# A fused attention and feed-forward kernel on eight cores: key matmul ahead of V's, the norm in two parts, and matmuls that nobody reads in some attention steps

## What is computed

```python
q = rms_norm(heads(x @ Wq), q_g)            # 16 heads of 64, 32 of them used in scores
kv = x @ Wkv                                # latent of 128
k = rms_norm(heads(kv @ Wk), k_g); v = heads(kv @ Wv)   # 32 per head
p = softmax(causal(q[..., :32] @ k.T / 8))
x = layernorm(x + pad(p @ v) @ Wo)
gate = silu(bitlinear(x, w_gate)); up = bitlinear(x, w_up)
x = layernorm(x + bitlinear(gate * up, w_down))
# bitlinear: activations to int8 per row, weights to -1, 0, 1 by their mean magnitude
```

## Time and profile before

| | us |
|---|---|
| three timed runs, median (lowest to highest) | 1638.44 (1637.69 to 1682.19) |
| the profiled execution, its own time | 1643.48 |
| its slowest core's span (core 6) | 1641.9 |
| spans of the eight cores | 1625.1 to 1641.9 |
| granted TensorE clock, mean of a core | 0.851 to 0.858 |

### The profile page before, as it was taken

The page is one execution under the profiler, slowest core; times in us unless marked ns, Lnnn a source line. Parts: engine busy times, 40 slices in busy tenths (PEclk is TensorE's granted clock), DMA queues, the critical chain, the costliest instruction groups (busy, mean ns, idle before and its releaser), DMA issues.

```text
span 1641.9 us, 22928 instructions; the slowest of 8 cores (1625.1 to 1641.9 us)
## 1 busy us (share of the span) xinstructions
PE 1302.4 (79%) x7494; PEld 438.3 (27%) x7494; DVE 806.2 (49%) x1158; ACT 824.7 (50%) x998; POOL 317.9 (19%) x350
## 2 busy tenths in 40 slices
PE   1676675788666888979869898989868999898966
PEld 0221121122111222222212222222223444343422
DVE  2227875468447766143561434143347762635522
ACT  2577564878784676657546686768601210111100
POOL 1024412033020304121123003130220020202021
PEclk8876686567556998989979998999989999898978
DMA  9995765779595785523255232523165585765646
GB/s 249 275 274 168 224 213 192 172 250 276 188 272 191 259 231 157 130 80 101 85 159 130 90 91 73 159 81 105 60 179 197 176 209 189 169 206 155 187 138 159
DMA packets 146514, 283.07 MB, mean 172 GB/s; under 512 B 91744, under 2 KB 92000, under 8 KB 133088
## 3 DMA queue, kind: packets, MB, share of 16 engines
q1 hardware_dynamic: 144816, 272.70, 54.6%
q0 software_dynamic: 1584, 8.91, 3.5%
HBM read 235.96 MB, written 33.55 MB: 164 GB/s over the span
## 4 chain that ended last, share of the span: by engine, by line
PE 51%; DVE 18%; issue 11%; ACT 8%; DMA 7%; POOL 3%; SPq 1%; DVEq 1%; ACTq 0%; POOLq 0%
PE ps_w L986 14%; PE ps_w L1109 6%; PE ps_sc L827 6%; ACT PT L840 5%; PE ps_den L782 4%; PE ps_sc L986 4%; PE ps_pv L793 3%; PE ps_sc L1109 3%; DVE S L775 3%; DMA R<-scr_w 2%; PE ps_w L547 2%; DVE st L690 2%; DMA R<-R 2%; DVE qb L382 2%; PE ps_w L714 2%
## 5 line engine op out<-in xcount | busy, mean ns | idle before, releaser
L840 ACT ACTIVATE PT<-ps_sc,negM 128x1024 bf16<-128x1024 f32 (+3 forms) x640 | 592.7, 983 | 197.6 <-PE ps_sc L827 195.3
L986 PE MATMUL ps_w<-R,S 128*128 128x512 fp8e4 x1280 | 336.1, 393 | 34.0 <-DVE R L1005 20.3
L827 PE MATMUL ps_sc<-qn,khat 32*128 32x512 bf16 (+3 forms) x1280 | 200.4, 397 | 63.5 <-ACT PT L840 58.7
L848 POOL TENSOR_TENSOR PT<-PT,tri 128x512 bf16<-128x512 bf16 x64 | 80.3, 1254 | 530.4 <-ACT PT L840 528.7
L986 PEld LDWEIGHTS ps_w<-R,S 128*128 128x128 bf16 x1280 | 106.4, 99 | 210.2 <-issue 121.0
L782 PE MATMUL ps_den<-PT,ones 128*32 128x512 bf16 (+3 forms) x1280 | 131.7, 402 | 18.4 <-DVE S L771 10.3
L853 POOL TENSOR_SCALAR PT<-PT,hflag_sb 128x512 bf16<-128x512 bf16 x64 | 112.9, 1763 | 111.0 <-ACT PT L840 110.9
L793 PE MATMUL ps_pv<-PT,vtok 128*32 128x512 bf16 (+3 forms) x1280 | 130.6, 398 | 0.1
L1109 PE MATMUL ps_w<-R 128*128 128x512 fp8e4 x416 | 114.2, 401 | 14.1 <-DMA R<-R 11.2
L986 PE MATMUL ps_sc<-R,S 128*128 128x512 fp8e4 x512 | 116.3, 386 | 8.8 <-DMA R<-scr_w 8.7
L1005 DVE SCALAR_TENSOR_TENSOR R<-R,ps_w 128x512 f32<-128x512 f32 x80 | 54.8, 685 | 137.2 <-ACT R L999 137.2
(11 more groups left out here) (182 smaller groups left out, 1379.2 us busy)
## 6 DMA issues: line engine op xcount, KB each, us to landing
R<-scr_w SPq DMA_DIRECT2D x192, 512.0 KB, 4.5
R<-wffn SPq DMA_DIRECT2D x69, 1024.0 KB, 7.6
scr_w<-qb SPq DMA_DIRECT2D x48, 256.0 KB, 6.6
khat<-wffn SPq DMA_DIRECT2D x9, 1024.0 KB, 15.0
vtok<-wffn SPq DMA_DIRECT2D x9, 1024.0 KB, 7.8
R<-xt POOLq DMA_DIRECT2D x7, 1024.0 KB, 13.7
R<-scr_x SPq DMA_DIRECT2D x12, 512.0 KB, 5.8
y<-R SPq DMA_DIRECT2D x12, 512.0 KB, 7.4
```

What stands on the lines that cost most here:

```text
L827: t = pe(lambda e, j=j, gi=gi, tc=tc, kc=kc, stc=stc: e.matmul(ps_sc[:, j * 512 + stc:j * 512 + 512], khat[32 * j:32 * j + 32, kc:kc + 128 ...
L840: t = act(lambda e, hf=hf, pp=pp, stc=stc: e.activation(PTr[pp][:, 2 * hf:2 * hf + 2, stc:512], PSr[:, 2 * hf:2 * hf + 2, stc:512], AF.Exp ...
L848: t = pool(lambda e, pp=pp, stc=stc: e.tensor_tensor(PTr[pp][:, :, stc:stc + 128], PTr[pp][:, :, stc:stc + 128], tri.rearrange("p (r n) -> ...
L986: t = pe(lambda e, c=c, b=b, kw=kk[w], i=i: e.matmul(wring.bufs[b], xqT[u % 2][:, i * 1024 + c * 128:i * 1024 + c * 128 + 128], wbuf[kw][: ...
```

## The change

Four edits in the program that writes the queues:

1. In `keys_values2` K's matmul and its squares come first and V's matmul behind it, in the same stage. V's copy to vtok is issued behind both.
2. In `projections` the last part of the job before (the writing of khat or qn, which frees the held bank) is issued ahead of the next job's first stage, where it stood behind it.
3. In `wo_ln1` the norm is split. The statistics are a piece of their own, and the normalization goes with the quantization. With two pieces per step, a row tile now takes four steps where it took three.
4. A helper `idle_mms` issues matmuls with the constant `bd32` on the first 512 columns of qn, into a free bank of `wring`, that nothing reads: four after each attention step that follows a stage of `keys_values2`, until the next stage of `queries2` or the one of `latent2` has run, and three per step between the end of the projections and the start of the feed-forward.

```diff
@@ keys_values2(c5, hc)
             kb = kvT[c5 % 2]
+            b1 = wring.take()
+            p1 = wring.bufs[b1]
+            t1 = pe(lambda e: e.matmul(
+                p1, wk[:, hc * 128:(hc + 1) * 128], kb, start=True, stop=True),
+                [t_kv[c5], wring.free[b1]], True)
+            t_sq = squares([(t1, p1)])
             b3 = wring.take()
             p3 = wring.bufs[b3]
-            t3 = pe(lambda e: e.matmul(
+            t3 = t_last[c5] = pe(lambda e: e.matmul(
                 p3, kb[:, hc * 128:(hc + 1) * 128], wv, start=True, stop=True),
-                [t_kv[c5], wring.free[b3]], True)
+                [wring.free[b3]], True)
...
             wring.give(b3, ends["v"])
-            b1 = wring.take()
-            p1 = wring.bufs[b1]
-            t1 = t_last[c5] = pe(lambda e: e.matmul(
-                p1, wk[:, hc * 128:(hc + 1) * 128], kb, start=True, stop=True),
-                [wring.free[b1]], True)
-            t_sq = squares([(t1, p1)])
             yield
@@ projections()
                 for _ in range(stages):
-                    next(job)
                     if old is not None:
                         next(old, None)
                         old = None
+                    next(job)
+                    st["few"] = stages == 2
                     yield
@@ wo_ln1(ti)
-            def norm1():
-                t_rs = layernorm_stats([state[0], state[1]], 0)
+            def stats():
+                state["rs"] = layernorm_stats([state[0], state[1]], 0)
+
+            def norm1_quant():
                 state["n"] = dve(lambda e: e.tensor_scalar(
-                    rt, rt, mv[:, 0:1], mv[:, 2:3], ALU.subtract, ALU.mult), [t_rs])
-
-            def quant():
+                    rt, rt, mv[:, 0:1], mv[:, 2:3], ALU.subtract, ALU.mult), [state["rs"]])
...
-            return [lambda: project(0), lambda: project(1), norm1, quant, None, store]
+            return [lambda: project(0), lambda: project(1), stats, None, norm1_quant, None, store,
+                    None]
@@ ahead of attention()
+        def idle_mms(n):
...
+            w = wring.take()
+            for _ in range(n):
+                pe(lambda e: e.matmul(wring.bufs[w], bd32[:], qn[:, 0:512], start=True,
+                                      stop=True), [wring.free[w]])
+            wring.give(w, wring.free[w])
@@ the main loop
         for part in attention():
             if not st["proj"]:
+                if st["few"]:
+                    idle_mms(4)
                 next(proj_it, None)
+            elif not ffn_on[0]:
+                idle_mms(3)
```

More of the change, by code:

```diff
@@ L311, in build_nc @@
         st = {"proj": False, "load": 0, "item": 0, "q": 0, "scl": None, "sum": [], "junk": None, "fi": None,
-              "mean": None}
+              "mean": None, "few": False}
         def stream_prefetch():
```

## The result

The changed kernel takes 1671.1 us (median of 4 runs, 1668.3 to 1713.9) where the one before takes 1641.4 (median of 4, the three above and one more). One execution of each kernel (1713.9 and 1682.2 us) was in a slower state of the chip, and the ratio leaves them out. It is 1.018, 95% interval 1.014 to 1.022: slower by about 30 us, where 1614 had been forecast, with a range up to 1640. The clock did rise as forecast: the cores' means lay between 0.851 and 0.858 and lie between 0.889 and 0.899 now. The time did not follow it.

A forecast was written before the change was run, and what follows sets the result against it. No engine was full over the whole span, so the bound was sought by stretch (ACT, DVE, or waits). Terms -8 - 12 + 2 - 3 + 3 + 9 - 7 - 8 = -24 us gave 1614 from the median 1638.4; range 1586 to 1640.

The forecast's parts named there:

- Edits 1 and 2: K and V jobs: K's matmul no longer waits for V's copy, so short waits go; -8 us, bounds 0 and 47.3.
- The third rival: K and V steps: the clock doesn't rise and PE becomes the bound; +13, 1651 us; chance 0.10.
- the wait changed its name: First rival, at K's matmul: it waits for khat instead of V's copy; total gain only -10, 1628 us; chance 0.27.
- inputs were ready a step earlier: At K's matmul: khat of the job before can be written without delay; ground for the -8 us.
- Edit 3, first tile: Stretch 260.9 to 299.5 us: the split norm ends 8.7 us of POOL waits and 3 us of blocks; -12 us.
- The wait of 8.80: K's matmul in the stretch of waits, with V's copy behind a norm on DVE; forecast to be gone.
- the last norm ahead of a chain: Pieces don't fit into 13 steps, so one norm runs right ahead of a chain; +2 us, bounds 0 and about 7.
- Edit 3, third tile: Feed-forward running, from step 204: 28 matmuls fall behind and are done alone after the attention; +3 us, bounds 0 and +7.
- Start of the feed-forward: Waits of 10.95 and 5.35 us for DVE at 527.13 and 540.85; half of 16.3 goes, -8 us, bounds 0 and -16.
- The gain of a warm start: Query matmuls and output projections after K and V parts start at full clock: 5 us and 2, together -7.
- The price: Unread matmuls at the low clock after about seven long DVE waits, one to two steps each: 7 x 1.3 = +9 us.
- at the full clock the fillers are hidden behind ACT or DVE: K and V steps with four fillers: 2.6 us of PE work per step against 3.8 us that ACT needs.

The follow-up runs named there:

- norm only: The kernel before with the split norm (edit 3) as its only change; ratio 0.995 (0.993 to 0.998), 1632.9 us.

## Why the prediction was wrong

**Edits 1 and 2: the failed step.** The prediction says "Edit 1 and 2, K's matmul first and khat's writing ahead. K's matmul now waits for khat of the job before". The edit in `projections` is made for every job, and I worked it out for one kind. Query and latent jobs had no reason to wait: their first matmuls used the free bank. Ahead of them the edit takes an overlap away and gives nothing. There was no term for it, nor a rival; it is 39 us (1671.1 against 1631.9 us with that part undone), and without it the change would have been faster, as forecast in sign, but by 8 us and not by 24. The third rival was slower too, at 1651, by a clock that stays low; the clock rose, so its reason isn't the one.

For the K and V jobs themselves I took -8 us; it was -3 (ratio 0.998), and the wait changed its name, 63.0 us for V's copy and khat to 59.4 for khat and qn. The argument that khat's "inputs were ready a step earlier" was wrong in some of the cases that it was made for: in eight of them DVE stood idle until ACT's exponential was done, 0.94 us ahead of K's matmul. In the long cases the inputs were ready and DVE was late, as I had said.

**Edit 3, first tile.** The wait of 8.80 isn't gone, but shorter: K's matmul at the same step waited 5.46 us with the norm alone (core 2) and 3.73 in the changed kernel. The one of 6.36, two steps ahead of it, became 0.94 with the norm alone. So this mechanism was right in kind. The POOL waits of the norms fell. The source of the norm's first instruction in the changed kernel (L730), then in the one before (L727):

```profile
  POOL mv L697: 9.8, 9
```

```profile
  POOL mv L696: 25.9, 16
```

Of the 12 us forecast, steps 34 to 49 gave 6.9 (norm only), and the last norm ahead of a chain cost 3.6 where I took 2. Together with the latent order that grew to 8.6: the profile shows DVE's block and the matmul that waited for its end (timeline of the changed kernel, DVE rows and a PE row):

```profile
310.70 1.27 DVE L691 BATCH_NORM_STATS2 st<-r_t 128x6 f32<-128x512 f32 x2
...
317.47 0.69 DVE L739 TENSOR_SCALAR S<-S 128x1024 bf16<-128x1024 f32 x1 [0.17 <-DVE S L737]
318.08 0.68 DVE L773 TENSOR_SCALAR S<-ps_den 128x512 f32<-128x512 f32 x1
...
323.34 0.68 DVE L582 TENSOR_TENSOR khat<-ps_w,S 128x512 bf16<-128x512 f32 x1
```

```profile
324.16 1.86 PE L528 MATMUL ps_w<-R 128*128 128x512 bf16 x4 [9.32 <-DVE khat L582]
```

The block runs from 310.70 to 324.0, and a latent's matmul, which in the old order would have run beside it, waited 9.32 us for its last instruction.

**Edit 3, third tile.** I forecast +3. With the norm alone, on core 0, steps 195 to 260 took 193.5 us instead of 218.3, steps 260 to 319 5.2 us more and what follows 6.4 more: -13 together. The eight cores lie between -3 and -16 there, with -7 in the middle; the sign holds on all of them, the size doesn't. That the 28 matmuls are done later fits the last two numbers. What I hadn't counted is the gain while they are missing. Whether it is the shorter DVE blocks or the steps without feed-forward work I didn't try apart.

**Start of the feed-forward.** Forecast -8. Steps 108 to 112 gave 8.6 us (norm only), and steps 112 to 124 took 8.4 back, since one of the norms now lies there: nothing.

**Edit 4.** The clock rose as expected, to 0.69 to 0.84 where it had been 0.50 to 0.60 in the table's stretches (0.83 from step 49 to 91, after 0.62 from 299.5 to 458 us), and the first query matmuls after K and V steps ran at 1.89 instead of 3.57. The gain of a warm start, taken as 7, was larger: with the unread matmuls alone -6.4 us at the queries on core 0 (-9.2 in the middle of the cores) where I took 5, and -6.9 at the feed-forward's start, which I had not counted; the 2 us of the last stretch ahead of it didn't come. The price, taken as +9, was 26 us, and the net +14 against +2. The failed step is "at the full clock the fillers are hidden behind ACT or DVE": it compared sums per step, 2.6 us of PE against 3.8 of ACT, and not the place. In steps 91 to 108, with three per step and PE's own work of 1.30, they cost 8.5 us as well, and 4.2 with one per step. I expect the waits of an output projection's additions and the low clock at the start of it to be the cause, and haven't tested that.

By the rule of the Trainium skill that I had set beside this ("TensorE: Matmul & The Clock Gate", "Part 1: The HAM clock gate"), a busy array gets the full clock. The traces agree: with the unread matmuls the mean was 0.885 to 0.897, and half as many left it at 0.863 to 0.872; all of them behind the stage, where they waited, left it at 0.862 to 0.874. What a full clock is worth is another question, and here it was worth less than its price. That there is nothing between the two levels holds in the traces of the kernel before and the changed one, but not in all: in the run with unread matmuls only ahead of the queries, cores 4 to 7 show a third one. A stretch of core 5, columns as in the earlier trace rows:

```profile
1248.00:1292.00 44.00, 44.00 (x169) 18.18 (x168) 31.98 (x55) 7.57 (x11) 0.77 (x2) 0.81 0.58 177
```

## What to carry to other kernels

When an edit changes the order for a loop over several kinds of jobs, each kind has to be worked out by itself: which buffer its first instruction asks for, and who must finish before that is free. With two buffers that are given out in turn, and one of them held, "free the old one first" can turn an overlap into a wait: the new job gets the buffer that has only just been given back. Filler work that is to keep a clock up belongs where no other engine waits for what stands behind it on the queue, and a full clock is worth only what the engine was late by.

## What I had not expected of the hardware

How far two traces with the same instructions agree depends on where one looks. Steps 64 to 73 took 26.7 us on core 0 in the kernel before and in all ten variants with its query order, and the kernel that was run twice (norm and K ahead of V) has the same time within 0.3 us in every group of the table up to step 73, and within 0.8 in the rest of the table. Behind it, with the feed-forward running, the same two traces differ by up to 2.0 us in a group, and steps 202 to 211 took 38.3 to 40.5 us on core 0 in the six kernels without the split norm, though 23.1 or 23.2 in all seven with it. So a difference of 2 us can be read from a single profile in the early groups, and not in the late ones. And half the unread matmuls did not give half the rise of the clock: 0.856 without, 0.867 with half, 0.89 with all of them.
